# Attention keys and queries kept whole in DRAM and split on chip one group ahead; rope from even and odd tiles; latents as two units

## What is computed

```python
xn  = layernorm(x)
c_q, c_kv = xn @ W_DQ, xn @ W_DKV              # 128 latent columns each
Qc, Kc, V = c_q @ W_UQ, c_kv @ W_UK, c_kv @ W_UV   # 16 heads of 32
Qr  = rope(c_q @ W_QR)                         # 16 heads of 16
Kr  = rope(xn @ W_KR)                          # 16, shared by the heads
Q, K = concat(Qc, Qr), concat(Kc, Kr)
p   = softmax(causal(clip(Q @ K.T, -80, 80)) / sqrt(48))
x   = x + (p @ V) @ W_O
x   = x + fp4_ffn(layernorm(x))                # gate, up, silu, down, 1408 wide
```

## Time and profile before

| what | value |
|---|---|
| median of 3 runs | 3206.03 us (3205.68 to 3207.39) |
| the profiled execution | 3209.62 us |
| its span, first to last instruction | 3207.7 us |
| granted TensorE clock, mean | 0.984 |
| PE busy | 3050.7 us (95%) |
| VectorE busy | 2603.6 us (81%) |
| ACT / POOL busy | 1222.5 / 659.2 us |
| projections | 0 to about 392 us |
| attention | 392 to about 1407 us |
| feed-forward | from 1407 us |
| HBM read, written | 205.55, 144.97 MB |

### The profile page before, as it was taken

The page is one execution under the profiler, slowest core; times in us unless marked ns, Lnnn a source line. Parts: engine busy times, 40 slices in busy tenths (PEclk is TensorE's granted clock), DMA queues, the critical chain, the costliest instruction groups (busy, mean ns, idle before and its releaser), DMA issues.

```text
span 3207.7 us, 65504 instructions
## 1 busy us (share of the span) xinstructions
PE 3050.7 (95%) x23492; PEld 2240.4 (70%) x23492; DVE 2603.6 (81%) x4428; ACT 1222.5 (38%) x1830; POOL 659.2 (21%) x633
## 2 busy tenths in 40 slices
PE   7999679999999999977999999999999999999999
PEld 6777534444444444446888888888888888888887
DVE  6777458888888888877888888888888888888886
ACT  3444346665666666652222222222222222222221
POOL 2434300000000000002323323323232232333322
PEclk9999889999999999988999999999999999999999
DMA  6999956566665756650000000000000000000000
GB/s 229 333 338 340 315 151 173 157 184 161 179 173 155 184 171 171 176 174 22 28 30 30 29 29 29 29 29 29 29 29 29 29 29 29 29 29 29 29 24 14
DMA packets 234506, 351.37 MB, mean 110 GB/s; under 512 B 17616, under 2 KB 117840, under 8 KB 234448
## 3 DMA queue, kind: packets, MB, share of 16 engines
q1 hardware_dynamic: 234448, 350.59, 35.7%
HBM read 205.55 MB, written 144.97 MB: 109 GB/s over the span
## 4 chain that ended last, share of the span: by engine, by line
PE 54%; DVE 1%; ACT 0%; POOL 0%; issue 0%; DVEq 0%
PE p_ring L1446 30%; PE p_ring L1474 15%; PE p_ring L1432 5%; PE p_ring L1464 2%; PE p_ring L1454 1%; DVE sb_fp_tmp L102 0%; DVE sb_xq L1347 0%; DVE sb_xq L104 0%; DVE sb_h_amax L88 0%; DVE sb_h L1358 0%; DVE sb_ht_lo L1376 0%; DVE sb_stats L1322 0%; DVE sb_xq L1339 0%; DVE sb_x L1320 0%; DVE sb_h L104 0%
## 5 line engine op out<-in xcount | busy, mean ns | idle before, releaser
L708 ACT ACTIVATE sb_probs<-scores 128x1024 f32<-128x1024 f32 (+3 forms) x768 | 586.1, 813 | 398.2 <-PE scores L886 386.2
L1446 PE MATMUL p_ring<-sb_wg_hi,sb_xq_hi 128*128 128x512 f32 (+1 forms) x1536 | 458.1, 379 | 0.0
L1446 PE MATMUL p_ring<-sb_wg_lo,sb_xq_hi 128*128 128x512 f32 (+1 forms) x1536 | 448.4, 373 | 0.0
L1446 PE MATMUL p_ring<-sb_wg_hi,sb_xq_lo 128*128 128x512 f32 (+1 forms) x1536 | 447.8, 373 | 0.0
L761 DVE TENSOR_SCALAR sb_probs<-sb_probs 128x2048 f32<-128x2048 f32 (+3 forms) x320 | 288.9, 903 | 91.7 <-ACT sb_probs L708 88.5
L901 PE MATMUL ps_o<-sb_probs,sb_v 128*32 128x512 f32 (+3 forms) x3072 | 328.2, 499 | 0.0
L1209 POOL TENSOR_TENSOR sb_h<-sb_h,sb_h_inv 128x512 f32<-128x512 f32 (+1 forms) x192 | 210.9, 1098 | 542.3 <-DVE sb_h_inv L94 542.3
L886 PEld LDWEIGHTS scores<-sb_q_hi,sb_k_hi 32*128 32x128 f32 x1536 | 74.0, 182 | 345.4 <-ACT sb_probs L708 284.3
L1446 PEld LDWEIGHTS p_ring<-sb_wg_hi,sb_xq_lo 128*128 128x128 f32 x1536 | 285.8, 188 | 41.5
L1446 PEld LDWEIGHTS p_ring<-sb_wg_lo,sb_xq_hi 128*128 128x128 f32 x1536 | 285.2, 188 | 41.2
L1446 PEld LDWEIGHTS p_ring<-sb_wg_hi,sb_xq_hi 128*128 128x128 f32 x1536 | 277.6, 189 | 35.8
(11 more groups left out here) (139 smaller groups left out, 5969.4 us busy)
## 6 DMA issues: line engine op xcount, KB each, us to landing
kq<-sb_kq_out SPq DMA_DIRECT2D x64, 1024.0 KB, 8.1
sb_xin<-in_L_attn_x_dram SPq DMA_DIRECT2D x32, 512.0 KB, 5.9
rq<-sb_r_out SPq DMA_DIRECT2D x32, 512.0 KB, 6.8
v<-sb_v_out SPq DMA_DIRECT2D x64, 256.0 KB, 6.0
sb_k_hi<-kq SPq DMA_DIRECT2D x32, 512.0 KB
sb_q_hi<-kq SPq DMA_DIRECT2D x32, 512.0 KB
sb_k_lo<-kq SPq DMA_DIRECT2D x32, 512.0 KB
sb_q_lo<-kq SPq DMA_DIRECT2D x32, 512.0 KB
```

The lines of the kernel that those rows point to most:

```text
L708: act.activation(probs[:, k % PROBS, 2 * pair:2 * pair + 2, off:BANK], scores[(2 * k + pair) % RING2][:, :, off:BANK], ACT.Exp, scale=SCAL ...
L1446: i = pe.matmul(ps[:, m, 0:b0 - a0], xt[a][:, c, :], wg[b][:, m, c, a0:b0], start=(c == 0 and a == b == 0), stop=(c == DC - 1 and a == 1))
```

## The change

In the projections: K and Q are copied from PSUM to `kq_out` unrounded and stored once (no lo, no L442). C becomes C0 (c_kv) and C1 (c_q) of 12 matmuls each. The rope queries come from two products, even columns and odd columns of W_QR (six matmuls in all, unit R, in place of R0 and R1); each 128x512 product is multiplied by two table planes in one VectorE instruction of 128x1024 outputs; POOL and ACT work on 128x1024. The table has four planes. PSUM slots are given back by two counters, ACT's (`act_free`: K, Q, V) and VectorE's (`dve_free`). VectorE no longer waits for the stores.

In attention: SP loads K and Q unsplit into one buffer `kq_raw` (two loads of 512 KB in place of four), after a wait that the buffer's last content has been split. ACT rounds them to hi behind its exponentials of steps 8 and 9 (k = 7 and 8), VectorE subtracts to get lo behind its clips of steps 10 and 11 (k = 9 and 10). PE waits for both lo parts ahead of `score` 0 of the next group.

```diff
-    c = np.repeat(cos, 2, axis=0)
-    s = np.repeat(sin, 2, axis=0)
-    s[0::2] *= -1.0
+    reps = P // (DR // 2)
+    turn = np.tile(np.concatenate([-sin, sin]), (P // DR, 1))
+    planes = [np.tile(-sin, (reps, 1)), np.tile(cos, (reps, 1)), np.tile(sin, (reps, 1)), turn]
...
-UNITS1 = ["C", "KR", "X0", "X1", "K0", "K1", "Q0", "Q1", "R0", "R1", "V0", "V1"]
+UNITS1 = ["C0", "C1", "KR", "X0", "X1", "K0", "K1", "Q0", "Q1", "R", "V0", "V1"]
...
+FREED_BY_ACT = ["K0", "K1", "Q0", "Q1", "V0", "V1"]
+FREED_BY_DVE = ["C0", "C1", "KR", "X0", "X1", "R"]
...
-        NW = O_QR + 512
+        NW = O_QR + 256
...
-        kq_out = sb("kq_out", [P, 2, 2, 2, 4, BANK])
+        kq_out = sb("kq_out", [P, 2, 2, 4, BANK])
...
+        def freed(eng, n, name):
+            if name in FREED_BY_ACT:
+                eng.wait_ge(act_free, (n + 1) * len(FREED_BY_ACT) + (FREED_BY_ACT.index(name) + 1))
+            else:
+                eng.wait_ge(dve_free, (n + 1) * len(FREED_BY_DVE) + (FREED_BY_DVE.index(name) + 1))
...
-                    for s in range(2):
-                        sp.dma_start(kq_v[k, s, b, :, :, cols], kq_out[:, half, k, s]).then_inc(stored[half], 16)
-                sp.wait_ge(rope_lo, n * 3 + 3 + 3)
+                    sp.dma_start(kq_v[k, b, :, :, cols], kq_out[:, half, k]).then_inc(stored[half], 16)
+                sp.wait_ge(rope_lo, n * 2 + 2 + 2)
                 for s in range(2):
-                    sp.dma_start(rq_v[s, b, :, :, cols], r_out[:, half, s]).then_inc(stored[half], 16)
+                    for c in range(2):
+                        sp.dma_start(rq_v[s, c, b, :, :, cols], r_out[:, half, s, c]).then_inc(stored[half], 16)
...
-                for k, name in enumerate(("KR", "R0", "R1")):
+                for k, name in enumerate(("KR", "R")):
...
-                        act.copy(c_hi[:], ps[:]).then_inc(act_hi, 1)
+                        act.copy(c_hi[:, int(name[1])], ps[:, 0]).then_inc(act_hi, 1)
...
-                        act.copy(kq_out[:, half, k, 0, 2 * m:2 * m + 2, :].bitcast(F32R), ps[:]).then_inc(act_hi, 1)
+                        act.copy(kq_out[:, half, k, 2 * m:2 * m + 2, :], ps[:]).then_inc(act_free, 1)
...
-                dve.wait_ge(stored[half], b * STORES1 + STORES1)
...
-                        dve.tensor_tensor(c_lo[:], ps[:], c_hi[:].bitcast(F32), ALU.subtract).then_inc(ps_free, 1)
-                        if not last:
+                        dve.tensor_tensor(c_lo[:, k], ps[:, 0], c_hi[:, k].bitcast(F32),
+                                          ALU.subtract).then_inc(dve_free, 1)
+                        if k == 1 and not last:
                             normalise(n + 1)
...
+                        dve.tensor_tensor(turned[:, 0], ps[:, 0, :].unsqueeze(1).to_broadcast([P, 2, BANK]),
+                                          rope[:, 1:3, pos], ALU.mult)
+                        dve.tensor_tensor(turned[:, 1], ps[:, 1, :].unsqueeze(1).to_broadcast([P, 2, BANK]),
+                                          rope[:, 0:2, pos], ALU.mult).then_inc(dve_free, 1)
...
-                        dve.tensor_tensor(kq_out[:, half, k, 1, pair, :], ps[:], kq_out[:, half, k, 0, pair, :],
-                                          ALU.subtract).then_inc(ps_free, 1)
...
-                get(k_hi[s][:], t["kq"][0, 0, heads].rearrange("i p t -> (i p) t"))
-                get(q_hi[s][:], t["kq"][1, 0, heads].rearrange("i p t -> (i p) t"))
-                get(k_lo[s][:], t["kq"][0, 1, heads].rearrange("i p t -> (i p) t"))
-                get(q_lo[s][:], t["kq"][1, 1, heads].rearrange("i p t -> (i p) t"))
+                sp.wait_ge(raw_split, g * 2 + 2)
+                for k in range(2):
+                    sp.dma_start(kq_raw[:, k], t["kq"][k, heads].rearrange("i p t -> (i p) t")).then_inc(raw_loaded, 16)
...
+            def round_raw(it2, s, k):
+                act.wait_ge(raw_loaded, it2 * 64 + (s * 32 + 32))
+                act.copy((k_hi, q_hi)[k][s][:], kq_raw[:, k]).then_inc(raw_rounded, 1)
...
+                    if k in (7, 8) and not last:
+                        round_raw(*following(it2, s), k - 7)
...
+            def rest_of_raw(it2, s, k):
+                dve.wait_ge(raw_rounded, it2 * 4 + (s * 2 + k + 1))
+                dve.tensor_tensor((k_lo, q_lo)[k][s][:], kq_raw[:, k], (k_hi, q_hi)[k][s][:].bitcast(F32),
+                                  ALU.subtract).then_inc(raw_split, 1)
...
+            dve.sem_inc(raw_split, 2)
+            rest_of_raw(0, 0, 0)
+            rest_of_raw(0, 0, 1)
             clip(0, 0, 0)
...
                     elif k == 9:
+                        if not last:
+                            rest_of_raw(*following(it2, s), 0)
...
                     elif k == 10:
+                        if not last:
+                            rest_of_raw(*following(it2, s), 1)
...
                 if k == 0:
                     pe.wait_ge(loaded[s], it2 * LOADS2 + LOADS2)
+                    pe.wait_ge(raw_split, it2 * 4 + (s * 2 + 2 + 2))
```

More of the change, by code:

```diff
@@ L228, in body @@
             def body(n, b, half, last):
-                units = units_of(last)
                 if not is_last(b):
@@ L270, in body @@
             def body(n, b, half, last):
-                units = units_of(last)
                 if not last:
                     inverse_deviation(n + 1)
-                for k, name in enumerate(("KR", "R0", "R1")):
+                for k, name in enumerate(("KR", "R")):
                     if name == "KR":
-                        tu = turned[0:DR, k]
-                        lo = kr_out[0:DR, half, 1, :]
-                        hi = kr_out[0:DR, half, 0, :]
-                    else:
[L280 to L288, removed]
+                        a, b_ = turned_kr[:, 0, :], turned_kr[:, 1, :]
+                        hi, lo = kr_out[0:DR, half, 0, :], kr_out[0:DR, half, 1, :]
+                    else:
+                        a, b_ = turned[:, 0], turned[:, 1]
+                        hi, lo = r_out[:, half, 0], r_out[:, half, 1]
+                    (freed_last if last else freed)(pool, n, name)
+                    pool.tensor_tensor(a, a, b_, ALU.add).then_inc(rope_sum, 1)
+                    pool.wait_ge(rope_hi, n * 2 + k + 1)
+                    pool.tensor_tensor(lo, a, hi, ALU.subtract).then_inc(rope_lo, 1)
             blocks(pool, body)
@@ L416, in body @@
                             normalise(n + 1)
-                    elif name in ("KR", "R0", "R1"):
-                        k = ("KR", "R0", "R1").index(name)
+                    elif name == "KR":
                         pos = slice(half * BANK, (half + 1) * BANK)
                         dve.wait_ge(ps_ready, number + 1)
[L422 to L430, removed]
-                    elif name[0] == "X":
[L432 to L441, removed]
-                        dve.tensor_tensor(kq_out[:, half, k, 1, pair, :], ps[:], kq_out[:, half, k, 0, pair, :],
-                                          ALU.subtract).then_inc(ps_free, 1)
@@ L475, in body @@
                 units = units_of(last)
-                his = [u for u in HI1 if u in units]
-                for name in units:
-                    number = unit(n, units.index(name))
+                for place, name in enumerate(units):
+                    number = unit(n, place)
                     ps = ring[slot(units, name)]
+                    if place >= RING1:
+                        before = units[place - RING1]
+                        (freed_last if last and before in FREED_BY_DVE else freed)(pe, n, before)
+                    else:
+                        freed(pe, n - 1, UNITS1[place - RING1])
                     if name[0] == "X":
@@ L493, in body @@
                     elif name[0] in "KQ":
-                        if name == "K0":
-                            pe.wait_ge(ps_free, unit(n, units.index("C")) + RING1 + 1)
+                        if name in ("K0", "Q0"):
+                            (freed_last if last else freed)(pe, n, "C0" if name == "K0" else "C1")
                         off, c = (O_UK, ckv) if name[0] == "K" else (O_UQ, cq)
```

114 lines of the change are left out of this document (67 added, 47 removed).

## The result

The changed kernel takes 3386.62 us (median of 4 runs, 3382.28 to 3391.10) against 3206.71: ratio 1.0564, interval 1.0551 to 1.0576. It is 180 us slower; 3286 was forecast, with a range of 3243 to 3340. The direction was right, the size was not: about 100 us are missing in the sum.

A forecast was written before the change was run, and what follows sets the result against it. PE was taken to bound the projections, and VectorE's trail to hold up PE at attention's group ends. From 3209.6: minus 31.4, 0.5 and 2.8, plus 86.8 and 28, gives 3289.7; the run median is 3.6 lower: 3286 us (3243 to 3340).

The forecast's parts named there:

- What bounds the kernel: PE sets the pace in projections, DMAs just keep up; in attention VectorE trails PE at a group's end.
- the projections: Fewer matmuls and a shorter chain to X0 gain 2.0 us for each of 15 bodies, together 31.4 us.
- POOL's chain: Projections: rope instructions of 1024 columns take 2.5 us each; 1/deviation ends 9.85 us after R, fitting with nothing to spare.
- Drain and first loads: Between projections and attention: drain of last stores changes 0, one MB less ahead of the values gains 2.8 us.
- ACT's copies cost nothing: Attention steps 9 and 10: exponentials start 0.5 and 0.3 us late, PE does not wait; cost 0.
- The pause: Before score 0 at each of 31 group boundaries PE waits 2.80 us for Q's lo, not paid back: +86.8 us.
- The clock term: After the pause PE's clock falls at half of the boundaries, 16, at 1.75 us each: +28 us (0 to 93).
- Rival 1: Attention boundaries: the pauses are there and the clock holds, 3258 us; chance 0.25.
- Rival 2: Attention boundaries: the clock falls at nearly every one, 3.0 us each, 3351 us; chance 0.10.
- Rivals 3 and 4: Attention boundaries: 3, stall only 1.7 us, 3224 us, chance 0.08; 4, split hidden behind PE's work, 3171 us, chance 0.07.

The follow-up runs named there:

- run 1: Changed kernel with 14 unread small matmuls on TensorE ahead of attention's first score, moving the loop about 55 instructions later: 3295.98 us.
- run 4: Changed kernel with the split moved to steps 2 and 3 and 14 small matmuls ahead of the attention loop: 3169.85 us, ratio 0.9883.
- run 3: Changed kernel with the split of K and Q moved to steps 2 and 3, TensorE's stream not moved: 3260.28 us, ratio 1.0168.
- places 0 and 11: Loop starts in instructions after the changed kernel's; split in steps 2 and 3 with 0 and 3 small matmuls: 3260.3 and 3263.0 us.
- places 182 and 183: Loop starts after the changed kernel's: kernel before with 32 small matmuls, 3269.75 us; split in steps 2 and 3 with 46, 3227.9 us.
- 27: Loop start 27 instructions after the changed kernel's: split in steps 2 and 3 with 7 small matmuls, 3168.8 us.
- 127: Loop start 127 instructions after the changed kernel's: split in steps 2 and 3 with 32 small matmuls, 3174.4 us (3169.0 and 3179.7).
- 315: Loop start 315 instructions after the changed kernel's: split in steps 2 and 3 with 79 small matmuls, 3170.0 us.

## Why the prediction was wrong

**What bounds the kernel, and the projections: right, a little small.** The body lost 2.20 us (2.0 taken); POOL's chain fitted as worked out (its instructions of 1024 columns take 2.42, 2.5 was taken), and VectorE starts on x 0.13 us after 1/deviation is there. Drain and first loads went as forecast: PE's last matmul to the first load is 15.8 us before and after, and the loads lost 2.2 us where 2.8 was taken. Without stall and reload the whole comes to 3206.4 - 3169.9 = 36.6 us against 34.7.

**ACT's copies cost nothing: right.** ACT in the changed kernel, against the earlier trace rows:

```profile
661.41 1.05 ACT L704 CAST sb_k_hi<-sb_kq_raw 128x1024 fp32r<-128x1024 f32 x1
662.35 1.52 ACT L725 ACTIVATE sb_probs<-scores 128x768 f32<-128x768 f32 x2
663.74 1.07 ACT L704 CAST sb_q_hi<-sb_kq_raw 128x1024 fp32r<-128x1024 f32 x1
664.68 1.11 ACT L725 ACTIVATE sb_probs<-scores 128x512 f32<-128x512 f32 x2
```

Counted from the start of their scores, step 9's exponentials (662.35) start 0.5 us later than before and step 10's 0.2 us. Score 10 starts 2.94 us after score 9, against 2.95 before, so PE lost nothing.

**The pause: right.** 2.84 us was measured and 2.80 forecast, one subtraction at 1.22 and the order as listed. It was not paid back: run 1's groups that kept the clock take 33.6 us. The busy share of VectorE fell from 83 to 76, though each group has more work for it: an engine with "room" was the one that PE waited for.

**The clock term: right in kind, too small.** 16 boundaries at 1.75 us were taken, 28 us. Measured: 126.1 - 31 x 2.83 = 38 us. The term's count was too low, 22 of the 30 inner intervals; its price came out right, 38 / 22 = 1.7, which is luck for a value taken between 0 and 3.0. Rival 1 has fallen: pauses of 2.83 us lost the clock at most boundaries, those of 1.64 never did. The rule that stood beside it (the Trainium skill, TensorE: Matmul & The Clock Gate, Why this matters for your kernels), by which short gaps between bursts keep the clock up, doesn't hold for these pauses of 2.83 us.

**The missing term: the reload, 90.5 us.** This is the step that failed. In attention the prediction added to a group's 30.70 us the pause and the clock alone, and from that expected groups of 33.5 us, or about 35. Whether TensorE's loop itself would still run as before was put at nothing, without a reason: the sum had no line for it, and no rival had it. Measured were 40.4 to 41.9 us at the 13 jumps. The loop's own instructions hardly changed (1705 in a turn against 1703). But the six matmuls taken out of each projection body (four bodies stand in the code), with smaller changes, moved the loop 54 instructions forward, out of a place where it stays resident; 55 instructions put back in run 1 undid that. With the reload the sum would have been 3286 + 90 = 3376, ten short of the measurement, about what the clock term lacked.

Could it have been seen? The trace of before has no instruction packet in the whole steady part of attention, though a turn of that loop is some 1700 instructions long on PE. So the loop was resident, and that could have been asked of the change. But no row of before says how near to an edge it stood; only the moved loops do.

**The ranking of rivals.** None reached the measurement. Rival 2 named 3351 for a clock lost everywhere; the late split alone is 3296. Rivals 3 and 4 fell with the pause. That the pause could be avoided was right in a form that the forecast didn't give: the idle time existed, but behind steps 2 and 3, not where the change had put the work.

## What to carry to other kernels

Work put on an engine with idle time costs what it delays: ask whether the idle time lies before or after the point at which someone waits. Here the same two copies and two subtractions cost 126 us at the group's end and nothing in steps 2 and 3. And when a long loop is left alone but code ahead of it changes, compare the instruction queue's packets before reading anything else. If they grew, move the loop and measure again, or a gain of 1.2% (run 4) looks like a loss of 1.7% (run 3).

## What the runs showed of the hardware

- This loop of some 1700 instructions on TensorE ran without an instruction packet, or with 9 packets of 16 KB at each jump back, according to its place in the stream. A jump with a reload cost 4.5 to 7.2 us: at places 0 and 11 it had two long stops and 6.8 us at half clock, at places 182 and 183 one long stop and at most 6.8 us at half clock. Moving the same loop by 16 instructions (from 11 to 27) took 94 us off the kernel.
- There are places at the edge: at 127, 2 of 13 jumps reloaded in the profiled execution, and its two executions differed by 10.7 us, where the two at 27 differ by 1.4 and the two at 315 by 0.1.
- TensorE's full clock was lost in none of 30 intervals with a pause of 1.64 us, and lost at 22 of 30 with 2.83 us and at 19 of 30 with 3.45 us.
